# Layer 1 expert feed-forward: exact matmuls of 128 columns replaced by three passes of 512 columns over halves of rows and weights

## What is computed

```python
raw_scores = einsum('bsd,ed->bse', u, centroids)             # 16 experts
s = softmax(raw_scores + expert_biases)
topk_vals, topk_idx = top_k(s, 2)
g_topk = sum(one_hot(topk_idx, 16) * topk_vals[..., None])   # 16 weights a row, 14 of them zero
xe = einsum('bsd,eod->bseo', u, Wr) + br                     # every expert for every row
routed = einsum('bse,bseo->bso', g_topk, xe)
shared = (einsum('bsd,eod->bso', u, Ws) + sum(bs)) / 2
x = x + tanh(g_ffn[1]) * (u + routed + shared)
```

## Time and profile before

| | us |
|---|---|
| median of 3 runs | 1948.7 |
| the runs | 1944.82, 1948.70, 1950.23 |
| span of the profiled execution, first to last instruction | 1942.7 |
| median of the runs less that span | 6.0 |
| first to last start of an expert matmul (L1984) | 975.3 to 1127.7 |

### The profile page before, as it was taken

One profiled execution on the slowest core, in us unless ns is written; L12 is line 12 of the kernel. 1 busy time (PEld: TensorE's weight loads), 2 busy tenths in 40 slices (PEclk: granted clock), 3 DMA queues, 4 the chain that ended last, 5 costly groups with the idle time before them and its releaser, 6 DMA issues. The chain is left out here.

```text
span 1942.7 us, 38924 instructions
## 1 busy us (share of the span) xinstructions
PE 1620.1 (83%) x12739; PEld 1206.0 (62%) x12739; DVE 1242.5 (64%) x3348; ACT 1210.7 (62%) x4192; POOL 740.3 (38%) x712
## 2 busy tenths in 40 slices
PE   4399999599999769999789966999579887866994
PEld 3355554379999546666589855545456555644994
DVE  5599999488888666767567755213457656654444
ACT  2189999189999557877667742433168656631444
POOL 2145555245555542111067835002222332333542
PEclk9799999699999889999889987999689888977997
DMA  3320000110000042423191022100044433313224
GB/s 127 74 106 1 1 1 1 34 45 2 1 2 2 28 116 76 105 72 89 32 320 54 1 88 86 42 0 1 19 121 114 124 101 84 88 55 97 70 70 156
DMA packets 63845, 126.40 MB, mean 65 GB/s; under 512 B 10670, under 2 KB 27233, under 8 KB 61529
## 3 DMA queue, kind: packets, MB, share of 16 engines
q1 hardware_dynamic: 53658, 103.10, 18.6%
q10 hardware_dynamic: 5616, 12.06, 1.9%
q0 software_dynamic: 4384, 8.89, 1.3%
HBM read 91.00 MB, written 50.43 MB: 73 GB/s over the span
## 5 line engine op out<-in xcount | busy, mean ns | idle before, releaser
L1531 ACT ACTIVATE L_E<-L_sc,L_negm 128x128 f32<-128x128 f32 x1024 | 300.1, 402 | 153.2 <-DVE L_negm L1399 152.5
L593 ACT ACTIVATE B_E<-B_logits,B_m 128x32 f32<-128x32 f32 (+1 forms) x1792 | 365.2, 374 | 8.8 <-DVE B_m L562 7.9
L599 POOL TENSOR_TENSOR B_E<-B_E,B_r 128x512 f32<-128x512 f32 x256 | 268.0, 1047 | 264.5 <-DVE B_r L581 264.5
L1399 DVE TENSOR_REDUCE L_negm<-L_sc 128x4 f32<-128x512 f32 x256 | 174.9, 686 | 87.0 <-PE L_sc L1640 74.9
L562 DVE TENSOR_REDUCE B_m<-B_logits 128x16 f32<-128x512 f32 (+1 forms) x256 | 172.8, 675 | 38.4 <-PE B_logits L553 31.2
L1638 PE MATMUL L_sc<-KS,L_QS 128*128 128x512 f32 x256 | 143.8, 562 | 54.5 <-DMA L_QS<-L_qsplit 37.1
L576 DVE TENSOR_REDUCE B_r<-B_E 128x16 f32<-128x512 f32 (+1 forms) x256 | 172.9, 675 | 2.5 <-POOL B_E L599 1.3
L1539 ACT ACTIVATE L_PT<-L_pt 128x512 f32<-128x512 f32 x256 | 165.9, 649 | 6.3 <-DMA picked_rows<-A_ys 6.0
L1648 PE MATMUL L_pt<-ident,L_E 128*128 128x128 f32 x1024 | 160.1, 280 | 0.8 <-ACT L_PT L1539 0.8
L551 PE MATMUL B_logits<-B_phihi,B_xhi 128*128 128x512 f32 x256 | 153.5, 600 | 5.1 <-DVE B_philo L538 2.5
L1648 PEld LDWEIGHTS L_pt<-ident,L_E 128*128 128x128 f32 x1024 | 126.6, 145 | 23.9 <-issue 2.5
(11 more groups left out here) (348 smaller groups left out, 3598.5 us busy)
## 6 DMA issues: line engine op xcount, KB each, us to landing
route_rows<-in_F_fill SPq DMA_DIRECT2D x33, 516.0 KB, 19.7
KS<-L_ksplit SPq DMA_DIRECT2D x180, 64.0 KB
L_QS<-L_qsplit SPq DMA_DIRECT2D x42, 256.0 KB
F_xg<-route_rows SPq DMA_DIRECT2D x71, 64.5 KB
ew<-in_expert_w SPq DMA_DIRECT2D x1, 4096.0 KB, 15.4
L_cT<-in_ctxT SPq DMA_DIRECT2D x16, 256.0 KB
L_qsplit<-L_qhi ACTq DMA_DIRECT2D x16, 256.0 KB, 2.7
L_qsplit<-L_qlo ACTq DMA_DIRECT2D x16, 256.0 KB, 5.8
```

The costliest lines, as they stand in the source:

```text
L593: ins = nc.scalar.activation(e[:, cols], self.bank(k)[:, cols], ACT.Exp, bias=self.m[:, k % 4, g:g + 1])
L599: self.st.nc.gpsimd.tensor_tensor(e, e, self.r[:, k % 2, :].unsqueeze(2) .to_broadcast([128, self.ng, self.size]), ALU.mult).then_inc(self ...
L1399: nc.vector.tensor_reduce(negm[:, k % 4, :], sc[k % 2][:].rearrange("p (h k) -> p h k", h=NHG), AX.X, ALU.max, negate=True).then_inc(s["ma ...
L1531: ins = nc.scalar.activation(e[:, h * 128:(h + 1) * 128], sc[k % 2][:, h * 128:(h + 1) * 128], ACT.Exp, bias=negm[:, k % 4, h:h + 1])
```

## The change

Only `stage_l1_ffn` is changed. Rows and expert weights are split into an upper half (rounded to float32r, tiles Whi and xhi) and the remainder (Wlo, xlo). A `product` is now one sequence j times four experts at once: three float32r matmuls with 512 moving columns, lower rows x upper weights, upper x lower, upper x upper, added up in one bank. There are still 16 banks' worth a group: for each j three given ones (experts 0 to 11, four PSUM banks `givenb`) and one own (experts 12 to 15, now one bank `ownb`).

- ACT splits the weights once, at the stage's start (4 instructions of 128x512) and the rows once a group (`upper`); it still scales quarters, 48 a group, but a quarter is now an expert.
- POOL makes Wlo (4 instructions of 128x512). In a group it adds the three parts of each j into `lanes` (2 adds x 4), and then folds the four expert lanes: one add of 128 x 4x256, one of 128x512 into `given`.
- DVE makes xlo (`lower`). Its four own instructions of one j now add into the same 128 columns of `acc`, each with a wait for the one before; the first reads xn in place of acc. The shared bank is added last in the group, not first.
- PE makes the shared bank during j = 2. It starts group n only when xlo of n is there, and the stage's first product only after Wlo.

```diff
-    NO, NA, RP, SH = NR // 4, NR - NR // 4, 6, 3
+    NQ, RP, RB = NR // 4, 6, 4
+    NA = NQ - 1
+    GIVEN, OWN, ADDS = NA * GB, 4 * GB, 2 * GB + 2
...
+        def lower(v, n, u):
+            v.wait_ge(s["x_hi"], n + 1)
+            nc.vector.tensor_tensor(xlo[u][:], front.xnT[u][:], xhi[u][:].bitcast(F32), ALU.subtract)\
+                .then_inc(s["x_lo"], 1)
...
# POOL
+            for i in range(NQ):
+                g.wait_ge(s["w_hi"], i + 1)
+                nc.gpsimd.tensor_tensor(Wlo[:, 4 * i:4 * i + 4, :], WrT[:, 4 * i:4 * i + 4, :],
+                                        Whi[:, 4 * i:4 * i + 4, :].bitcast(F32), ALU.subtract).then_inc(s["w_lo"], 1)
             def group(n, u, first, more):
+                for j in range(GB):
+                    g.wait_ge(s["given_used"], n * GIVEN + NA * j + 2 + RB)
+                    g.wait_ge(s["given_added"], n * ADDS + 2 * j + ADDS)
+                    nc.gpsimd.tensor_tensor(lanes[:, j, :], part[NA * j % RP][:], part[(NA * j + 1) % RP][:], ALU.add)\
+                        .then_inc(s["given_added"], 1)
...
+                    nc.gpsimd.tensor_tensor(lanes[:, j, :], lanes[:, j, :], part[(NA * j + 2) % RP][:], ALU.add)\
+                        .then_inc(s["given_added"], 1)
+                    if j == 2 and not first:
+                        tail.gpsimd(g, n - 1, 1 - u)
+                g.wait_ge(s["given_added"], n * ADDS + 2 * GB + ADDS)
+                nc.gpsimd.tensor_tensor(lanes[:, :, 0:256], lanes[:, :, 0:256], lanes[:, :, 256:512], ALU.add)\
+                    .then_inc(s["given_added"], 1)
                 g.wait_ge(s["given_taken"], n + 1)
...
+                nc.gpsimd.tensor_tensor(given[u][:].rearrange("p (a o) -> p a o", a=GB), lanes[:, :, 0:128],
+                                        lanes[:, :, 128:256], ALU.add).then_inc(s["given_added"], 1)
...
# DVE
+            def own(n, u, j):
+                v.wait_ge(s["own_ready"], n * GB + j + 1)
+                for e in range(4):
+                    if e:
+                        v.wait_ge(s["own_used"], n * OWN + 4 * j + e + 4)
+                    before = acc[u][:, j, :] if e else front.xn[u][:, j, :]
+                    nc.vector.scalar_tensor_tensor(acc[u][:, j, :], db[:, e * 128:(e + 1) * 128],
+                                                   rt.G[u][:, j, NA * 4 + e:NA * 4 + e + 1], before,
+                                                   ALU.mult, ALU.add).then_inc(s["own_used"], 1)
...
             def group(n, u, first, more):
                 if more:
                     front.vector(v, n + 1, 1 - u)
+                own(n, u, 0)
                 if not first:
                     finish(n - 1, 1 - u)
+                own(n, u, 1)
                 if more:
+                    lower(v, n + 1, 1 - u)
                     rt.choose(v, n + 1, steps)
+                own(n, u, 2)
                 if more:
                     rt.weigh(v, n + 1, 1 - u, steps)
+                own(n, u, 3)
+                add_shared(n, u)
...
# ACT
                 a.wait_ge(rt.G_ready, n + 1)
+                for j in range(GB):
+                    a.wait_ge(s["given_added"], n * ADDS + 2 * j + (8 if j >= 2 else 6))
+                    for q in range(NA):
+                        k = NA * j + q
+                        a.wait_ge(s["given_ready"], n * GIVEN + k + 1)
+                        for c in range(4):
+                            ins = nc.scalar.activation(part[k % RP][:, c * D:(c + 1) * D], ab[k % RB][:, c * D:(c + 1) * D],
+                                                       ACT.Copy, scale=rt.G[u][:, j, 4 * q + c:4 * q + c + 1])
+                        ins.then_inc(s["given_used"], 1)
...
# PE
+            def product(u, q, j, bank):
...
+                nc.tensor.matmul(bank[:], xlo[u][:, cols], hi_w, start=True, stop=False)
+                nc.tensor.matmul(bank[:], xhi[u][:, cols], lo_w, start=False, stop=False)
+                return nc.tensor.matmul(bank[:], xhi[u][:, cols], hi_w, start=False, stop=True)
...
+            def own_of(n, u, j):
+                t.wait_ge(s["own_used"], n * OWN + 4 * j + 4)
+                product(u, NA, j, db).then_inc(s["own_ready"], 1)
...
             def group(n, u, more):
+                t.wait_ge(s["x_lo"], n + 1)
+                rt.tensor_turn(t, n, u)
+                for j in range(GB):
+                    given_of(n, u, j, 0)
+                    given_of(n, u, j, 1)
+                    own_of(n, u, j)
+                    given_of(n, u, j, 2)
+                    if j == 0 and more:
                         front.tensor(t, n + 1, 1 - u)
+                    if j == 1 and more:
                         t.wait_ge(front.xnT_ready, n + 3)
                         rt.tensor(t, n + 1, front.xnT[1 - u])
+                    if j == 2:
+                        shared(n, u)
```

122 lines of the change are left out of this document (54 added, 68 removed).

## The result

| | before | after |
|---|---|---|
| median of 4 runs each | 1946.76 us | 1964.91 us |
| the runs | 1939.33 to 1950.23 | 1961.27 to 1974.69 |
| ratio, 95% interval | | 1.0118 [1.0094, 1.0142] |
| span of the profiled execution | 1942.7 | 1972.8 (its time: 1974.69) |

The change makes the kernel slower by 1.2%, 18 us by the medians. The forecast was 1966.6 us, slower.

What follows compares the result with a forecast made beforehand. PE bounds the kernel before; after, DVE's normalising meeting POOL's fold makes the period 21.7 us. Start +0.4, six periods +15.6 and end +1.9 sum to +17.9 on 1948.7: 1966.6 us, range 1945 to 1976.

Steps and rivals of the forecast that it cites:

- The bound of before: Middle group of the kernel before: PE leads, busy 18.0 of 19.4 us at full granted clock, by about 3 us.
- The walk through the middle group: Middle group followed from the end of own 2: the normalising meets POOL's fold, 6.4 us for 1.0; period 21.7 us.
- The price of the fold: POOL's fold of 1024 elements, shown by no row, taken as twice an add of half as many: 2.6 us.
- single hindrances: DVE's single waits on POOL in a group (means, xlo, subtraction, G): about 1.0 us.
- The rival that POOL does not catch the normalising: DVE normalises before POOL's last add: 4.4 us for 6.4, period 19.7, 1955 us; or as now, 1949; chance 0.24.
- The rival of a small hindrance: Faster case: DVE's instructions slip into POOL's pauses, period 17.0 us, -10.3 us, 1938 us; chance 0.15.
- The own chain: DVE's four own instructions of one j, now dependent: 4 x 0.38 = 1.52 us for 1.04.
- The 11 us that hung on that price: At 0.26 us per own instruction the own work would not grow, and the time would be some 11 us lower.
- The start: Stage start: first product 4.4 us later, but group 0 is short in return, so own 2 ends only +0.4 us.
- The end: From own 2 of group 6 to the last `finish`: near 26.1 us for 24.2, +1.9.
- the same ring: Experiments' later theory: DVE frees the own bank, PE fills it, ACT and POOL follow through the fold, needed before own 1.
- The clock: Rival: PE at half speed after each 5 us pause, period 22.5 us, +22.7 us, 1971 us; chance 0.11.

Runs made afterwards that it cites:

- the second look: The changed kernel measured again without any edit, against the kernel before on the same chip: 1963.59 us, ratio 1.0114, stage 195.8 us.

## Why the prediction was right, and where it was not

**The bound of before** held. Given the same move of the normalising, the kernel before gained nothing, as it should where PE leads (17.98 of 19.60 us busy at full clock).

**The walk through the middle group** held step by step as far as own 0. Zero, the end of own 2, is at 1037.49 in the group shown above (four starts from 1035.98, 0.386 apart, and 0.35):

| event | forecast | measured |
|---|---|---|
| own 3 begins | 1.1 | 1.06 |
| shared addition begins | 2.6 | 2.66 |
| normalising begins | 3.3 | 3.27 |
| POOL's last add | 3.0 to 4.3 | 3.05 to 4.35 |
| fold ends | 6.9 | 6.78 |
| given addition ends | 8.3 | 8.12 |
| next first add ends, own 0 can begin | 9.7 | 9.47 |

The price of the fold, taken as twice an add, was 2.36 for 2.6. "One normalising instruction passes per POOL instruction" is what the four blocks above show. The Trainium skill, "SBUF — State Buffer", section "Who interferes with whom", has the two engines exclude each other for the whole instruction; the trace agrees, and with the fold's 2.36 us it shows it for an instruction almost twice as long as those of before.

Not all groups had all four blocked: blocks of 4.91 and 5.3 stand beside 6.3 and 6.5, 5.8 on average for the 6.4 of the walk. What the walk put too high there came back in terms it had too low. In the six periods xlo took 0.9 on average and not 0.7, X in `finish` 1.18 and not 0.75, the router's L1790 0.60 and not 0.23. These read two SBUF operands; the small copies L1777 and L200, which read one, took up to 1.25 in place of 0.17. All such single hindrances add 2.2 us a group where the walk had 1.0. Two errors of 0.6 down and 1.2 up nearly cancel in the period, and that is luck. The single hindrances fall unevenly, too: the group shown has few of them, the one of 24.0 us had L1790 at 1.33, L200 at 1.25 and L1777 at 1.24.

The rival that POOL does not catch the normalising asked for 4.4 or less; no block in the two looks was below 4.91. The rival of a small hindrance is out by the same numbers.

**The own chain.** Forecast 1.52 for four, measured 1.51. The Trainium skill, "VectorE: DVE Perf Modes", TRN2 errata, has 120 + columns cycles for a PSUM source; the trace agrees for independent instructions (0.26 us apart, in the kernel that made them so) but not for this chain, 0.386 apart, where each waits for a semaphore of the one before. The 11 us that hung on that price were not there. The experiment gives the chain 7.3 us of the stage and 6.5 of the median.

**The start.** The result was near (+1.0 for +0.4), the step in it was not. The first expert product came 15.4 us after the stage's start for 8.8 before, +6.6 and not +4.4. In order of time, ACT, POOL and PE of the kernel after:

```profile
972.05 2.19 ACT L1972 ACTIVATE F_Whi<-F_WrT 128x512 fp32r<-128x512 f32 x4 [3.02 <-DMA F_WrT<-in_L1F_WrT]
972.76 5.58 POOL L1874 TENSOR_TENSOR F_Wlo<-F_WrT,F_Whi 128x512 fp32r<-128x512 f32 x4 [7.20 <-ACT F_Whi L1972]
...
980.31 0.39 PE L1808 MATMUL F_route<-ident,F_G 128*64 128x128 f32 x1 [9.49 <-DVE F_G L1795]
980.45 0.79 PE L2013 MATMUL F_givenb<-F_Whi,F_xlo 128*128 128x512 f32 x1
```

The weights were ready at 978.34; what PE then still waited for was G, since `tensor_turn` now stands ahead of the first product, a step of the moved order that the forecast had left out. Group 0 made up for most of it: from the first product to the end of own 2 it took 13.4 us, and the forecast had 15.0. That the two errors cancel is luck as well.

**The end is the term that was mis-sized:** +8.6 for +1.9 (+6.7 in the second look). The steps that the prediction names add up to 25.5 us and not to its 26.1, so that they give +1.3. The prediction walked from group 6 to the last `finish` through PE's five products at full clock and one wait for POOL. The trace of after shows what it left out. DVE:

```profile
1135.93 0.69 DVE L1924 TENSOR_TENSOR F_acc<-F_acc,F_given 128x512 f32<-128x512 f32 x1 [2.62 <-POOL F_given L1894]
...
1144.07 0.35 DVE L1936 SCALAR_TENSOR_TENSOR F_acc<-F_ownb,F_G,F_xn 128x128 f32<-128x128 f32 x1 [1.74 <-PE F_ownb L2015]
...
1150.82 0.35 DVE L1936 SCALAR_TENSOR_TENSOR F_acc<-F_ownb,F_G,F_xn 128x128 f32<-128x128 f32 x1 [5.24 <-PE F_ownb L2015]
...
1158.28 0.69 DVE L1924 TENSOR_TENSOR F_acc<-F_acc,F_given 128x512 f32<-128x512 f32 x1 [5.15 <-POOL F_given L1894]
```

PE:

```profile
1142.38 0.79 PE L2013 MATMUL F_ownb<-F_Whi,F_xlo 128*128 128x512 f32 x1 [5.87 <-DVE F_acc L1936]
1142.97 0.63 PE L2014 MATMUL F_ownb<-F_Wlo,F_xhi 128*128 128x512 f32 x1
1143.40 0.63 PE L2015 MATMUL F_ownb<-F_Whi,F_xhi 128*128 128x512 f32 x1
```

In the last group nothing is normalised, so DVE is at `finish` early and waits 2.62 us for the fold of group 6. PE stands 5.87 us for the one own bank, which own 1 behind `finish` must free, and comes back with passes 0.43 us apart; two products and the shared bank go through at that pace, and own 3 begins at 1150.82 after a wait of 5.24. Counted from the end of own 2, `finish` began at 10.5 for the 8.3 of the forecast, own 1 ended at 16.8 for 13.4, and the last `finish` began at 32.8 for 26.1. It is the same ring as in the kernel with the normalising on ACT: take the block on DVE away, and `finish`, the one bank and the slow PE stand behind it. Two own banks take 6.6 us off this stretch.

**Why the sum still came close.** The stage grew by 26.6 (23.7 in the second look) for a forecast of 17.9, the median by 18.2 (21.4 on the chip of the second look). The median lies in the range and near the forecast, but 6 to 9 us of the stage are under-forecast, 5 to 7 of them in the end. That the first pair of medians hides this is luck; why the rest of the program scatters was not looked for.

**The clock** was put down as a rival with 0.11 and is partly in what happened: granted 0.84 in the middle group, 0.74 in the last, full speed before. The Trainium skill, "TensorE: Matmul & The Clock Gate", Part 1, has an idle array fall back to half rate; the trace agrees, half rate behind each pause of 4 to 6 us. But it does not set the length of the middle groups. Four of the six periods of the kernel after, columns as above:

```profile
1037.49:1058.41 20.92, 16.13 (x66) 12.61 (x66) 18.95 (x55) 13.26 (x47) 12.55 (x9) 0.84 0.00 0
1058.41:1082.36 23.95, 18.10 (x78) 13.58 (x76) 21.75 (x55) 15.80 (x57) 17.17 (x14) 0.93 0.00 0
1082.36:1103.05 20.69, 15.90 (x66) 12.44 (x66) 18.78 (x55) 13.56 (x49) 12.55 (x9) 0.84 0.00 0
1103.05:1125.47 22.42, 15.84 (x71) 12.41 (x70) 20.24 (x53) 14.28 (x52) 15.33 (x13) 0.92 0.01 1
```

The two with the lowest granted clock are the shortest of all six, and the length goes with DVE's busy time. What the clock costs where PE's own bank is on the path, in the last group and in the kernels with the normalising on ACT, was not separated.

**What the prediction thought too simple** is that the block on the normalising is a cost by itself. It is one of two ways in which the fold's delay reaches own 1, and moving it to ACT alone gave back 0.5 us of the 2.6 by which the period of the second look exceeds that of before.

## What to carry to other kernels

When two engines use a resource in turn and one of them reads it behind a step that needs a third engine's sum, shorten the sum first: here folding the partial sums as they come, in small pieces, gave back 16 of the stage's 24 us, while moving the blocked work to another engine gave 3. Walk the last group apart from the middle ones, since the work that covered a wait there is missing. And before an instruction is put on VectorE that reads two SBUF tiles, look at what GpSimd runs back to back at that moment: each one may last as long as GpSimd's.

## What was unexpected of the hardware

- Between two POOL instructions 0.07 us apart, exactly one DVE instruction gets in. An L124 whose record begins 0.03 us before that of POOL's add was still blocked (6.53 us, four instructions).
- POOL loses as well: its add of 128x512, 1.27 us, took 1.6 to 1.8 in single places where DVE's two-SBUF instruction ran first (the kernel with the normalising on ACT, 1064.56 and 1066.42).
- POOL's addition is not in proportion to its size: 0.46 us for 128 columns, 0.74 for 256, 1.27 for 512, 2.36 for 1024. Spreading the fold costs POOL 1.2 us a group, and pays.
- ACT's copy to float32r of 128x512 took 0.63 us, and its four normalising instructions, from SBUF to SBUF, 1.65 without ever a block, where DVE's took 1.12 to 6.5.
